# A graph attention layer on one core: the accumulators start without a product for rows that have no edge

## The chip, the cores and the metric

One core of a Trainium2 chip runs the whole layer. The metric is the device time in microseconds (us) of one execution. Before the change it is 1485.84 us, the median of three runs (1485.68 to 1487.18).

## The reference

```
h = maximum(layernorm(x), 0)                    # x: 8192 x 256, float32
Wh = h @ W_w + W_b                              # 256 x 256
e = leaky_relu((Wh @ a1)[:, None] + (Wh @ a2)[None, :], 0.2)
attention = softmax(where(adj > 0, e, -9e15), axis=1)   # adj: 8192 x 8192, int32, 0 or 1
out = x + attention @ Wh
```

A row of `adj` without a single 1 has the same value in all its columns, so its softmax is uniform and its output is x plus the mean of Wh over all 8192 nodes. Of the 8192 columns about 32 in each row hold a 1.

## The kernel before

**Names.** The 8192 output rows are handled in 8 blocks (`s`, `NS`) of 1024, each as `M` = 8 tiles (`m`) of 128 rows. The 8192 neighbours are summed over in 32 units (`k`, `NK`) of 256, each as two halves (`e`) of 128. A chunk (`g`) is 8 units, so a block has 4 chunks. The adjacency of a chunk is loaded in 8 sets, so a block has 32 sets too; set `n` of all 256 goes into slot `n % 12` of `rows8` (`R8` = 12).

**Before the blocks** (the first 100 us), x is loaded, normalised (VectorE finds the factors, GpSimd multiplies by them at L279, each 128 x 256 float32), transposed and multiplied by W on TensorE, and stored as `X16`: two float16 parts, high and low, of Wh (without its bias) times a factor of the column, with that factor in a 257th column. TensorE also forms the mean of h W (L781), and VectorE turns it into `mean` (L643 to L647).

**In the blocks**, four engines pass a unit on. ScalarE forms the products `Wt` (L362, twice 128 x 1024). VectorE applies the lower bound and the adjacency (`weights`, L656, 128 x 2048 float32, both tensor inputs in SBUF). ScalarE writes the high float16 part into `Et` (`high`, L377). VectorE writes the low part (`low`, L663, 128 x 2048, both tensor inputs in SBUF). TensorE then runs 48 products of 128 x 128 by 128 x 257 (L789): 8 tiles, 2 halves, 3 combinations of high and low parts. `Et` and `Wt` are rings of 4 units, so ScalarE's `high` waits until TensorE has read the unit four back. VectorE also transposes one set of adjacency bytes per unit (L586, 128 x 512 int32, one input), always 8 or more sets ahead of the unit that uses it.

**The order on each engine is fixed.** VectorE in a usual chunk: `weights` of the next unit, `low` of this one, a transpose. At a chunk's end its last two transposes stand together. At the first chunk of a block the order is written out (`chunk_after_last`): transposes of sets 8 and 9 of the block, `finish` of the first four tiles of the block before, `weights`, `finish` of the other four, `weights`, `low`, the transpose of set 10, and so on. `finish` (L667) takes reciprocals of the 257th column of the accumulators (L671) and adds each accumulator times its reciprocal to x in `xr` (L674, one input in PSUM and one in SBUF), a tile at a time.

**TensorE** holds the 8 accumulators in the 8 banks of PSUM. The first two and the last two units of a block go tile by tile, so that VectorE can read tile 0 while tile 1 is still being summed; before the first product into a tile, TensorE waits for VectorE's reading of it (`s_ev`) and then runs `start` (L793): a product of the constant `tiny` by `mean`, which puts 2^-100 times the mean into the accumulator and its denominator. So a row without an edge ends as the mean, and no denominator is zero.

**GpSimd** in the blocks issues the loads of the adjacency in order: `load_adj(n)` (L285, four DMAs) waits for the transpose of set n - 12, whose slot it fills. After set 27 of a block it issues the two DMAs that add the bias to `xr` (L295), each after a wait for the load of `xr`. **SyncE's queue** stores the two halves of `xr` of the last block when VectorE has read the accumulators, and loads the next x rows into `xr` when the store has landed.

Of the kernel before, what the change touches and what calls it, by code (L numbers as in the profile page):

```python
# [14 lines left out]
P = 128  # L15
# [14 lines left out]
def gat_layer(nc, x, adj, W_w, W_b, a, out):  # L30
# [48 lines left out]
    with ctx:  # L79
# [9 lines left out]
        rows8 = sb("adj_rows8", [P, R8, SQ, 4 * QP * CW], U8)  # L89
        cols8 = sb("adj_cols8", [P, 2, CW, R, 4], U8)  # L90
        xr = sb("xr", [P, 2, H, F], F32)
        tiny = sb("tiny", [P, P], BF16)
        mean = sb("mean_wh", [P, F2], F16)
        r_j = sb("r_j", [P, NB], F32)
        r_2 = r_j[:, :].rearrange("p (k e) -> p k e", e=2)
        c_j = sb("c_j", [P, NB], F32)
# [23 lines left out]
        newt = scratch[:, 1552:1568]  # L120
        rstd = scratch[:, 1568:1632]
        shift = scratch[:, 1632:1696]
        mean_hi = scratch[:, 1696:1824].bitcast(F16)
        s_t = scratch[:, 1824:1952].rearrange("p (b n) -> p b n", n=2)
        t_top = scratch[:, 1952:1984]
        t_fac = scratch[:, 1984:2016]
        h_sum = sb("h_sum", [P, KF], F32)
        mean_f = sb("mean_f", [P, F], F32)
        Wx = q_odd[:, 0:KF * F2].rearrange("p (k f) -> p k f", k=KF)
        bias = q_odd[:, KF * F2:(KF + 1) * F2]  # L130
        ident = q_odd[:, (KF + 1) * F2:(KF + 1) * F2 + P]
# [69 lines left out]
        s_fin = sem("acc_complete")  # L201
        s_rden = sem("rden_ready")
        s_ev = sem("acc_read")

# [4 lines left out]
        @block.sync  # L211
        def _(sp):
            def load_x(g):
                k, lo, hi, b = GROUPS[g]
                xk = x_in[:, k * Y:(k + 1) * Y, :].rearrange("p (w e) f -> p w (e f)", e=4)
                for q in range(NQ):
                    sp.dma_start(xk[QP * q:QP * (q + 1), lo:hi], x_cols[q, k][:, lo:hi]).then_inc(s_x[g], 16)

            load_x(0)
            for k in range(KF):  # L220
                sp.dma_start(Wx[:, k, 0:F], W_w[k * P:(k + 1) * P, :]).then_inc(s_par, 16)
            for k in range(2):
                sp.dma_start(a_row[:, k, :], a[k * F:(k + 1) * F, :].rearrange("f o -> o f").broadcast_to([P, F])).then_inc(s_par, 16)
            for g in range(1, len(GROUPS)):
                load_x(g)
            sp.dma_start(bias[:, 0:F], W_b.rearrange("(o f) -> o f", o=1).broadcast_to([P, F])).then_inc(s_bias, 16)

            def load_q(s):
                sp.dma_start(q_bc[s % 2], q_dram.ap()[s:s + 1, :].broadcast_to([P, R])).then_inc(s_q, 16)

            def load_xr(s, half):
                sp.dma_start(xr[:, half], x_rows[s, half]).then_inc(s_xr[half], 16)

            def store(s, half):
                sp.dma_start(out_rows[s, half], xr[:, half]).then_inc(s_out[half], 16)

            def store_q(q, lo, hi, done):
                sp.dma_start(q_store[q][:, lo:hi], q_j[QP * q:QP * (q + 1), 4 * lo:4 * hi].rearrange("p (z e) -> p z e", e=4)).then_inc(done, 16)

            NZ = NC * CW  # L240
            sp.wait_ge(s_qn, 1)
            store_q(0, 0, NZ // 2, s_q0)
            sp.wait_ge(s_q0, 16)
            load_q(0)
            store_q(0, NZ // 2, NZ, s_qst)
            for q in range(1, NQ):
                store_q(q, 0, NZ, s_qst)
            sp.wait_ge(s_qst, 16 * NQ)
            sp.wait_ge(s_X, NB)
            sp.wait_ge(s_mean, 1)  # L250
            for s in range(NS):
                if s + 1 < NS:
                    sp.wait_ge(s_W, NK * s + 1)
                    load_q(s + 1)
                if s:
                    for half in range(2):
                        sp.wait_ge(s_ev, M * s - H * (1 - half))
                        store(s - 1, half)
                for half in range(2):
                    if s:  # L260
                        sp.wait_ge(s_out[half], 16 * s)
                    load_xr(s, half)
            for half in range(2):
                sp.wait_ge(s_ev, M * NS - H * (1 - half))
                store(NS - 1, half)
            for half in range(2):
                sp.wait_ge(s_out[half], 16 * NS)

        @block.gpsimd
        def _(pool):  # L270
            nc.gpsimd.memset(ident, 0.0).then_inc(s_ident, 1)
            pool.wait_ge(s_ident, 1)
            nc.gpsimd.affine_select(out=ident, in_=ident, compare_op=ALU.not_equal, fill=1.0, base=0,
                                    pattern=[[-1, P]], channel_multiplier=1).then_inc(s_ident, 1)

            def normalise(b):

                pool.wait_ge(s_norm, GROUP[b] + 1)
                nc.gpsimd.tensor_scalar(x_in[:, b, :], x_in[:, b, :], rstd[:, b:b + 1], shift[:, b:b + 1],  # L279
                                        ALU.mult, ALU.add).then_inc(s_hp, 1)  # L280

            def load_quadrant(n, q):

                s, k, m = n // NSET, n % NSET // SETS, n % SETS
                pool.dma_start(rows8[QP * q:QP * (q + 1), n % R8], adj_v[s, m, k, q]).then_inc(s_rows[n % R8], 16)  # L285

            def load_adj(n):
                if n >= R8:
                    pool.wait_ge(s_T, n - R8 + 1)
                for q in range(NQ):  # L290
                    load_quadrant(n, q)

            def add_bias(s, half):
                pool.wait_ge(s_xr[half], 16 * s + 16)
                pool.dma_start(xr[:, half], W_b.rearrange("(o m f) -> o m f", o=1, m=1).broadcast_to([P, H, F]),  # L295
                               accum_op=ALU.add).then_inc(s_xb[half], 16)

            for b in range(4, NB):
                normalise(b)
                turn, at = divmod(b - 4, 3)  # L300
                if at < 2 and 2 * turn + at < NQ * SETS:
                    load_quadrant(*divmod(2 * turn + at, NQ))
            pool.wait_ge(s_q, 16)
            for n in range(SETS, NSET * NS):
                load_adj(n)
                if n % NSET == 2 * R8 + 3:
                    for half in range(2):
                        add_bias(n // NSET, half)
# [111 lines left out]
        def _(dve):  # L420
# [5 lines left out]
                dve.wait_ge(s_chain, steps[0])  # L426

            nc.vector.memset(ones, 1.0).then_inc(s_ones, 1)
            nc.vector.memset(tiny[:, :], TINY)
            step(nc.vector.memset(mean[:, :], 0.0))  # L430

            def stats(g, lo, hi):

# [206 lines left out]
            step(nc.vector.tensor_copy(X16[:, :, 0, F], c_j[:, :]))  # L640
            nc.vector.tensor_tensor(X16[:, :, 1, F], c_j[:, :], X16[:, :, 0, F], ALU.subtract).then_inc(s_den, 1)
            dve.wait_ge(s_tot, 1)
            nc.vector.tensor_copy(mean[0:1, F:F1], sc[0:1, 8:9])  # L643
            step(nc.vector.tensor_scalar(mean_f[:, :], ps_mean[:, 0:F], sc[:, 8:9], None, ALU.mult))
            step(nc.vector.tensor_copy(mean_hi, mean_f[:, :]))
            nc.vector.tensor_copy(mean[0:1, 0:F], mean_hi[0:1, :])
            nc.vector.tensor_tensor(mean[QP:QP + 1, 0:F], mean_f[QP:QP + 1, :], mean_hi[QP:QP + 1, :], ALU.subtract).then_inc(s_mean, 1)  # L647

            def weights(g, i):

# [15 lines left out]
            def finish(s, half):  # L666
# [1 line left out]
                lo = H * half  # L668
                dve.wait_ge(s_fin, M * s + (lo + H))
                dve.wait_ge(s_xb[half], 16 * s + 16)  # L670
                nc.vector.reciprocal(rden[:, lo:lo + H], acc[:, lo:lo + H, F]).then_inc(s_rden, 1)  # L671
                dve.wait_ge(s_rden, 2 * s + (half + 1))
                for m in range(lo, lo + H):
                    nc.vector.scalar_tensor_tensor(out=xr[:, half, m - lo, :], in0=acc[:, m, 0:F], scalar=rden[:, m:m + 1],  # L674
# [53 lines left out]
                    chunk(g)  # L728
            for half in range(2):
                finish(NS - 1, half)  # L730

        @block.tensor
        def _(pe):
# [50 lines left out]
            pe.wait_ge(s_X, NB)  # L784
            pe.wait_ge(s_den, 1)

            def part(m, k, e, n, last=False):

                return nc.tensor.matmul(acc[:, m, 0:F1], Et[:, 2 * (k % RING) + e, 1 if n == 2 else 0, m * P:(m + 1) * P],  # L789
                                        X16[:, 2 * k + e, 1 if n == 1 else 0, 0:F1], start=False, stop=last)  # L790

            def start(m):
                nc.tensor.matmul(acc[:, m, 0:F1], tiny[:, :], mean[:, 0:F1], start=True, stop=False)  # L793

            def first_units(s):

                pe.wait_ge(s_E, NK * s + 2)
                for m in range(M):
                    pe.wait_ge(s_ev, M * s + (m + 1 - M))
                    start(m)  # L800
                    for k in range(2):
                        for e in range(2):
                            for n in range(3):
                                ins = part(m, k, e, n)
                ins.then_inc(s_pe, 1)

            def unit(s, k):
                pe.wait_ge(s_E, NK * s + (k + 1))
                for e in range(2):
                    for m in range(M):  # L810
                        for n in range(3):
                            ins = part(m, k, e, n)
                return ins

            def last_units(s):

                pe.wait_ge(s_E, NK * s + NK)
                for m in range(M):
                    for k in range(NK - 2, NK):
                        for e in range(2):  # L820
                            for n in range(3):
                                ins = part(m, k, e, n, k == NK - 1 and e == 1 and n == 2)
                    ins.then_inc(s_fin, 1)

            for m in range(M):
                start(m)
            unit(0, 0)
            unit(0, 1).then_inc(s_pe, 1)
            for s in range(NS):
# [25 lines left out]
```

## Time and profile before

| | |
|---|---|
| median of three runs | 1485.84 us |
| profiled execution | 1486.66 us |
| its span, first to last instruction | 1484.9 us |
| TensorE matmul busy | 1450.0 us (98%) |
| VectorE busy | 1421.7 us (96%) |
| ScalarE busy | 1086.0 us (73%) |
| GpSimd busy | 605.4 us (41%) |
| mean granted TensorE clock | 0.992 of full speed |

Busy shares are unions of the recorded durations. VectorE's instructions overlap by a little at their ends, and matmuls by more, so the distance between two starts, and not the duration, says what one costs its engine.

### The profile page before, as it was taken

How to read it: one execution, taken by the hardware profiler on the slowest of the kernel's cores; microseconds unless marked ns; L12 is line 12 of the kernel's file. 1: busy time of each engine (PE TensorE's matmuls, PEld its weight loads, DVE VectorE, ACT ScalarE, POOL GpSimd, SP SyncE). 2: the span in 40 equal slices, each digit the busy share in tenths (PEclk: the TensorE clock that was granted, in tenths of full speed). 3: DMA queues.
4: the chain of work that ended last, by engine and by line, in shares of the span. 5: the costliest groups of instructions: out<-in, count | busy, mean ns of one | idle time of the engine just before them, and what ended most of it. 6: DMA issues, size and time to landing. Idle time of an engine off the chain costs nothing.

```text
span 1484.9 us, 29899 instructions
## 1 busy us (share of the span) xinstructions
PE 1450.0 (98%) x12746; PEld 1261.6 (85%) x12746; DVE 1421.7 (96%) x1263; ACT 1086.0 (73%) x1006; POOL 605.4 (41%) x1106
## 2 busy tenths in 40 slices
PE   6969999999999999999999999999999999999998
PEld 5848888888888888888888888888888888888887
DVE  8989999999999999999999999999999999999993
ACT  4768888687777777687776877777776877777771
POOL 4748444354443444354442544344432544433000
PEclk9989999999999999999999999999999999999999
DMA  9729997798778977799777977699677887788000
GB/s 215 86 26 131 98 73 55 108 82 61 51 65 102 84 51 51 85 97 69 52 64 95 86 53 51 60 117 75 48 61 102 77 61 51 51 102 70 2 1 29
DMA packets 179559, 107.53 MB, mean 72 GB/s; under 512 B 20065, under 2 KB 176353, under 8 KB 179425
## 3 DMA queue, kind: packets, MB, share of 16 engines
q0 software_dynamic: 155904, 75.56, 68.1%
q1 hardware_dynamic: 23520, 30.05, 6.9%
q8 instruction: 100, 1.64, 0.4%
q14 instruction: 35, 0.28, 0.1%
HBM read 298.45 MB, written 8.42 MB: 207 GB/s over the span
## 4 chain that ended last, share of the span: by engine, by line
PE 81%; DVE 15%; DMA 1%; issue 1%; POOL 0%; SPq 0%; ACT 0%; DVEq 0%
PE acc L789 80%; DVE work L663 4%; DVE work L656 4%; DVE xr L437 1%; DVE adj_cols L586 1%; DVE X L489 1%; DMA adj_rows<-in_adj 1%; PE acc L756 1%; PE acc L793 0%; DVE xr L448 0%; DVE xr L484 0%; DMA work<-q_rows 0%; POOL adj_rows L285 0%; DVE xr L473 0%; DVE xr L469 0%
## 5 line engine op out<-in xcount | busy, mean ns | idle before, releaser
L789 PE MATMUL acc<-X,work 128*128 128x257 f16 x12288 | 1367.6, 273 | 7.1 <-DVE work L663 7.1
L789 PEld LDWEIGHTS acc<-X,work 128*128 128x128 f16 x12288 | 1189.8, 97 | 178.8 <-DVE work L663 7.6
L285 POOL DMA_DIRECT2D adj_rows<-in_adj x1024 | 551.3, 548 | 721.4 <-DVE adj_cols L586 684.8
L377 ACT ACTIVATE work<-work 128x2048 f16<-128x2048 f32 x256 | 488.0, 1909 | 292.2 <-PE acc L789 269.8
L663 DVE SCALAR_TENSOR_TENSOR work<-work 128x2048 f16<-128x2048 f32 x256 | 585.3, 2286 | 26.6 <-ACT work L377 26.5
L656 DVE SCALAR_TENSOR_TENSOR work<-work,sigma,adj_cols 128x2048 f32<-128x2048 f32 x256 | 595.1, 2325 | 5.7 <-ACT work L362 2.2
L362 ACT ACTIVATE work<-q_odd,r_j 128x1024 f32<-128x1024 f32 x256 | 278.5, 1135 | 23.9 <-DVE work L663 23.9
L362 ACT ACTIVATE work<-work,r_j 128x1024 f32<-128x1024 f32 x256 | 278.5, 1136 | 23.4 <-DVE work L663 18.2
L586 DVE STREAM_TRANSPOSE adj_cols<-adj_rows 128x512 int32<-128x512 int32 x256 | 177.1, 701 | 1.4 <-DMA adj_rows<-in_adj 1.4
L756 PE MATMUL acc<-q_odd,adj_cols 128*128 128x258 f32 x256 | 64.4, 396 | 0.7 <-ACT adj_cols L329 0.6
L756 PEld LDWEIGHTS acc<-q_odd,adj_cols 128*128 128x128 f32 x256 | 48.0, 197 | 8.7 <-ACT adj_cols L329 2.1
L279 POOL TENSOR_SCALAR work<-work,xr 128x256 f32<-128x256 f32 x60 | 33.6, 564 | 32.4 <-DVE xr L464 31.3
L747 PE MATMUL acc<-q_odd,work 128*128 128x128 f32 x128 | 21.5, 289 | 13.2 <-ACT work L320 9.9
L747 PEld LDWEIGHTS acc<-q_odd,work 128*128 128x128 f32 x128 | 16.2, 146 | 18.4 <-issue 11.9
L437 DVE BATCH_NORM_STATS2 xr<-work 128x6 f32<-128x256 f32 x64 | 25.4, 417 | 3.9 <-DMA work<-in_x 3.7
L489 DVE SCALAR_TENSOR_TENSOR X<-acc,c_j,X 128x256 f16<-128x256 f32 x64 | 28.6, 473 | 0.0
L334 ACT ACTIVATE c_j<-xr 128x2 f32<-128x2 f32 x32 | 9.5, 296 | 25.8 <-DVE xr L484 25.3
L674 DVE SCALAR_TENSOR_TENSOR xr<-acc,rden,xr 128x256 f32<-128x256 f32 x64 | 26.6, 478 | 0.6
L339 ACT ACTIVATE X<-acc,c_j 128x256 f16<-128x256 f32 x64 | 26.8, 476 | 0.0
L329 ACT ACTIVATE adj_cols<-acc 128x256 f32<-128x256 f32 x64 | 23.4, 369 | 0.1
L295 POOL DMA_DIRECT2D xr<-in_L_gnn_W_b x16 | 21.4, 1622 | 1.0 <-issue 1.0
L793 PE MATMUL acc<-mean_wh,tiny 128*128 128x257 f16 x64 | 17.2, 291 | 2.8 <-DVE mean_wh L647 1.6
(76 smaller groups left out, 84.4 us busy)
## 6 DMA issues: line engine op xcount, KB each, us to landing
adj_rows<-in_adj POOLq DMA_DIRECT2D x1024, 64.0 KB, 4.2
xr<-in_x SPq DMA_DIRECT2D x16, 512.0 KB, 4.6
xr<-in_L_gnn_W_b POOLq DMA_DIRECT2D x16, 512.0 KB, 17.0
out<-xr SPq DMA_DIRECT2D x16, 512.0 KB, 5.4
work<-in_x SPq DMA_DIRECT2D x28, 256.0 KB, 15.1
work<-q_rows SPq DMA_DIRECT2D x4, 512.0 KB, 5.4
q_odd<-q_rows SPq DMA_DIRECT2D x4, 512.0 KB, 5.7
work<-in_x SPq DMA_DIRECT2D x8, 128.0 KB, 3.3
```

The costliest lines, as they stand in the source:

```text
L279: nc.gpsimd.tensor_scalar(x_in[:, b, :], x_in[:, b, :], rstd[:, b:b + 1], shift[:, b:b + 1], ALU.mult, ALU.add).then_inc(s_hp, 1)
L285: pool.dma_start(rows8[QP * q:QP * (q + 1), n % R8], adj_v[s, m, k, q]).then_inc(s_rows[n % R8], 16)
L362: ins = nc.scalar.mul(Wt[:, i % RING, e, :], q_bc[s % 2], r_j[:, 2 * k + e:2 * k + e + 1])
L377: nc.scalar.mul(Et[:, at:at + 2, 0, :], Wt[:, i % RING], SCALE).then_inc(s_H, 1)
L437: nc.vector.bn_stats(st[:, b % XG + n, :], x_in[:, b + n, :]).then_inc(s_bn, 1)
L489: nc.vector.scalar_tensor_tensor(out=X16[:, b, 1, 0:F], in0=ps_wh[:, b % WH, 0:F], scalar=c_j[:, b:b + 1], in1=X16[:, b, 0, 0:F], op0=ALU. ...
L586: nc.vector.transpose(rows.rearrange("p w (q r) -> p q w r", q=SQ), rows8[:, n % R8].bitcast(I32).rearrange("p q (w c) -> p q w c", w=CW)) ...
L656: nc.vector.scalar_tensor_tensor(out=slot, in0=slot, scalar=sigma[:, k:k + 1], in1=edges, op0=ALU.max, op1=ALU.min).then_inc(s_M, 1)
L663: nc.vector.scalar_tensor_tensor(out=Et[:, at:at + 2, 1, :], in0=Wt[:, i % RING], scalar=SCALE, in1=Et[:, at:at + 2, 0, :], op0=ALU.mult, ...
L747: ins = nc.tensor.transpose(ps_hT[p % 2][:, (2 * c + e) * P:(2 * c + e + 1) * P], x_in[:, b, c * P:(c + 1) * P], ident)
L756: ins = nc.tensor.matmul(ps_wh[:, b % WH, 0:F2], hT[:, p % 2, c, e * P:(e + 1) * P], Wx[:, c, :], start=(c == 0), stop=(c == KF - 1))
L789: return nc.tensor.matmul(acc[:, m, 0:F1], Et[:, 2 * (k % RING) + e, 1 if n == 2 else 0, m * P:(m + 1) * P], X16[:, 2 * k + e, 1 if n == 1 ...
```

## The change

`tiny` and the products of `start` (8 before the first block, 8 in each of the other seven) go. The first product into each accumulator now carries the start flag. `finish` raises the denominator to at least 2^-100, notes in `none` which rows had no edge, and takes the reciprocal of the raised value. GpSimd, after the loads of set 21 of the next block, takes the mean times `none` for each tile into `part_mean` and adds that to `xr`; the store waits for it. In the last block VectorE adds the mean itself after its `finish`. The mean is a plain float32 copy of TensorE's result, where five instructions stood.

```diff
@@ sync
-                        sp.wait_ge(s_ev, M * s - H * (1 - half))
+                        sp.wait_ge(s_mn, M * s - H * (1 - half))
                         store(s - 1, half)
@@ gpsimd
+            def add_mean(s):
+                pool.wait_ge(s_mean, 1)
+                for m in range(M):
+                    pool.wait_ge(s_ev, M * s + m + 1)
+                    if M * s + m:
+                        pool.wait_ge(s_mn, M * s + m)
+                    nc.gpsimd.tensor_scalar(part_mean[:, :], mean[:, :], none[:, m:m + 1], None, ALU.mult).then_inc(s_pm, 1)
+                    pool.wait_ge(s_pm, M * s + m + 1)
+                    nc.gpsimd.tensor_tensor(xr[:, m // H, m % H, :], xr[:, m // H, m % H, :], part_mean[:, :], ALU.add).then_inc(s_mn, 1)
...
                 load_adj(n)
+                if n >= NSET and n % NSET == R8 + 9:
+                    add_mean(n // NSET - 1)
@@ vector
-            nc.vector.memset(tiny[:, :], TINY)
-            step(nc.vector.memset(mean[:, :], 0.0))
...
-            nc.vector.tensor_copy(mean[0:1, F:F1], sc[0:1, 8:9])
-            step(nc.vector.tensor_scalar(mean_f[:, :], ps_mean[:, 0:F], sc[:, 8:9], None, ALU.mult))
-            step(nc.vector.tensor_copy(mean_hi, mean_f[:, :]))
-            nc.vector.tensor_copy(mean[0:1, 0:F], mean_hi[0:1, :])
-            nc.vector.tensor_tensor(mean[QP:QP + 1, 0:F], mean_f[QP:QP + 1, :], mean_hi[QP:QP + 1, :], ALU.subtract).then_inc(s_mean, 1)
+            nc.vector.tensor_copy(mean[:, :], ps_mean[:, 0:F]).then_inc(s_mean, 1)
@@ finish
-                nc.vector.reciprocal(rden[:, lo:lo + H], acc[:, lo:lo + H, F]).then_inc(s_rden, 1)
+                step(nc.vector.tensor_scalar(rden[:, lo:lo + H], acc[:, lo:lo + H, F], TINY, None, ALU.max))
+                if s:
+                    dve.wait_ge(s_mn, M * s + (lo + H - M))
+                nc.vector.tensor_scalar(none[:, lo:lo + H], rden[:, lo:lo + H], TINY, None, ALU.is_equal)
+                nc.vector.reciprocal(rden[:, lo:lo + H], rden[:, lo:lo + H]).then_inc(s_rden, 1)
@@ after the last finish
             for half in range(2):
                 finish(NS - 1, half)
+                dve.wait_ge(s_ev, M * NS - H * (1 - half))
+                for m in range(H * half, H * half + H):
+                    nc.vector.scalar_tensor_tensor(out=xr[:, half, m - H * half, :], in0=mean[:, :], scalar=none[:, m:m + 1],
+                                                   in1=xr[:, half, m - H * half, :], op0=ALU.mult, op1=ALU.add).then_inc(s_mn, 1)
@@ tensor
-            def start(m):
-                nc.tensor.matmul(acc[:, m, 0:F1], tiny[:, :], mean[:, 0:F1], start=True, stop=False)
...
-                    start(m)
-                                ins = part(m, k, e, n)
+                                ins = part(m, k, e, n, first=(k == 0 and e == 0 and n == 0))
...
-            for m in range(M):
-                start(m)
```

## Rows read from the trace of the kernel before

**Rows 1.** Waits: engine line <- what ended the wait: us in total, times, longest.
```profile
ACT work L377 <- PE acc L789: 269.8, 190, 4.2
...
PE acc L789 <- DVE work L663: 7.1, 1, 7.1
...
PE acc L793 <- DVE xr L674: 1.2, 1, 1.2
```

**Rows 2.** The chain that ended last: start us, us, what.
```profile
183.19 1.23 DVE adj_cols L586 x2
...
223.88 1.22 DVE adj_cols L586 x2
...
293.92 160.64 PE acc L789 x1452
454.67 1.33 PE acc L789 x12
456.10 1.33 PE acc L789 x12
```

**Rows 3.** Timeline (start us, us, what, [idle before]), block 0 to block 1.
```profile
282.13 0.71 DVE L586 STREAM_TRANSPOSE adj_cols<-adj_rows 128x512 int32<-128x512 int32 x1
...
282.75 0.15 DVE L671 RECIPROCAL rden<-acc 128x4 f32<-128x4 f32 x1
282.94 1.66 DVE L674 SCALAR_TENSOR_TENSOR xr<-acc,rden,xr 128x256 f32<-128x256 f32 x4
283.13 2.15 POOL L285 DMA_DIRECT2D adj_rows<-in_adj  x4 [5.18 <-DVE adj_cols L586]
...
283.57 0.27 PE L793 MATMUL acc<-mean_wh,tiny 128*128 128x257 f16 x1 [1.20 <-DVE xr L674]
...
284.51 2.34 DVE L656 SCALAR_TENSOR_TENSOR work<-work,sigma,adj_cols 128x2048 f32<-128x2048 f32 x1
...
286.77 0.18 DVE L671 RECIPROCAL rden<-acc 128x4 f32<-128x4 f32 x1
...
288.56 2.35 DVE L656 SCALAR_TENSOR_TENSOR work<-work,sigma,adj_cols 128x2048 f32<-128x2048 f32 x1
...
293.02 0.71 DVE L586 STREAM_TRANSPOSE adj_cols<-adj_rows 128x512 int32<-128x512 int32 x1
```

**Rows 4.** Timeline, VectorE, block 1: the `low` of unit 15.
```profile
353.10 2.29 DVE L663 SCALAR_TENSOR_TENSOR work<-work 128x2048 f16<-128x2048 f32 x1
```

**Rows 5.** Timeline, VectorE, block 2: the transposes of sets 22 and 23.
```profile
518.86 1.30 DVE L586 STREAM_TRANSPOSE adj_cols<-adj_rows 128x512 int32<-128x512 int32 x2
```

**Rows 6.** One line, GpSimd's normalising: duration ns min/median/max, first and last start.
```profile
L279 POOL TENSOR_SCALAR work<-work,xr x60: 544/553/1176, 15.2 to 83.6; 128x256 f32<-128x256 f32 x60
```

**Rows 7.** Timeline before the blocks: GpSimd beside VectorE with two inputs in SBUF.
```profile
29.06 0.58 POOL L279 TENSOR_SCALAR work<-work,xr 128x256 f32<-128x256 f32 x1
29.28 0.38 DVE L471 TENSOR_TENSOR xr<-xr 128x8 f32<-128x8 f32 x1
...
30.48 0.16 DVE L471 TENSOR_TENSOR xr<-xr 128x8 f32<-128x8 f32 x1
...
73.50 1.18 POOL L279 TENSOR_SCALAR work<-work,xr 128x256 f32<-128x256 f32 x1
...
73.57 0.42 DVE L573 CUSTOM_DVE_ANT_0 X<-q_odd,xr 128x256 f32<-128x256 f32 x1
...
73.91 0.42 DVE L573 CUSTOM_DVE_ANT_0 X<-q_odd,xr 128x256 f32<-128x256 f32 x1
```

**Rows 8.** Timeline, GpSimd's first steps: one waits for the other.
```profile
0.74 0.21 POOL L271 MEMSET q_odd<- 128x128 f32 x1 [0.29 <-POOLq L845]
1.19 0.29 POOL L273 TENSOR_SCALAR_AFFINE_SELECT q_odd<-q_odd 128x128 f32<-128x128 f32 x1 [0.24 <-POOL q_odd L271]
```

**Rows 9.** DMA issues: KB each, median us from issue to landing.
```profile
adj_rows<-in_adj POOLq DMA_DIRECT2D x1024, 64.0 KB, 4.2
```

**Rows 10.** Timeline: the end.
```profile
1479.77 1.66 DVE L674 SCALAR_TENSOR_TENSOR xr<-acc,rden,xr 128x256 f32<-128x256 f32 x4
```

More of the change, by code:

```diff
@@ L91, in gat_layer @@
         xr = sb("xr", [P, 2, H, F], F32)
-        tiny = sb("tiny", [P, P], BF16)
-        mean = sb("mean_wh", [P, F2], F16)
+        none = sb("rows_without_edge", [P, M], F32)
+        part_mean = sb("part_mean", [P, F], F32)
         r_j = sb("r_j", [P, NB], F32)
@@ L122, in gat_layer @@
         shift = scratch[:, 1632:1696]
-        mean_hi = scratch[:, 1696:1824].bitcast(F16)
         s_t = scratch[:, 1824:1952].rearrange("p (b n) -> p b n", n=2)
@@ L127, in gat_layer @@
         h_sum = sb("h_sum", [P, KF], F32)
-        mean_f = sb("mean_f", [P, F], F32)
+        mean = sb("mean_hw", [P, F], F32)
         Wx = q_odd[:, 0:KF * F2].rearrange("p (k f) -> p k f", k=KF)
@@ L203, in gat_layer @@
         s_ev = sem("acc_read")
+        s_pm = sem("mean_part_ready")
+        s_mn = sem("means_added")
         NPE = NK - 3
@@ L263, in _ @@
             for half in range(2):
-                sp.wait_ge(s_ev, M * NS - H * (1 - half))
+                sp.wait_ge(s_mn, M * NS - H * (1 - half))
                 store(NS - 1, half)
@@ L785, in _, with part @@
             pe.wait_ge(s_den, 1)
-            def part(m, k, e, n, last=False):
+            def part(m, k, e, n, first=False, last=False):
                 return nc.tensor.matmul(acc[:, m, 0:F1], Et[:, 2 * (k % RING) + e, 1 if n == 2 else 0, m * P:(m + 1) * P],
-                                        X16[:, 2 * k + e, 1 if n == 1 else 0, 0:F1], start=False, stop=last)
-            def start(m):
-                nc.tensor.matmul(acc[:, m, 0:F1], tiny[:, :], mean[:, 0:F1], start=True, stop=False)
+                                        X16[:, 2 * k + e, 1 if n == 1 else 0, 0:F1], start=first, stop=last)
             def first_units(s):
@@ L811, in unit @@
                         for n in range(3):
-                            ins = part(m, k, e, n)
+                            ins = part(m, k, e, n, first=(s == 0 and k == 0 and e == 0 and n == 0))
                 return ins
@@ L821, in last_units @@
                             for n in range(3):
-                                ins = part(m, k, e, n, k == NK - 1 and e == 1 and n == 2)
+                                ins = part(m, k, e, n, last=(k == NK - 1 and e == 1 and n == 2))
                     ins.then_inc(s_fin, 1)
-            for m in range(M):
-                start(m)
             unit(0, 0)
```

## The prediction, made before the changed kernel was run

> **What bounds the kernel now.** I read the waits first. TensorE waits for VectorE once at the start of the blocks (7.1 us) and once for `finish` (1.2 us), and never again [rows 1]; ScalarE waits 269.8 us for TensorE to free its ring. So TensorE bounds blocks 1 to 7. The chain of waits says the same, and shows what it costs: in the middle of a block 1452 products take 160.64 us, 110.6 ns each; at the start of a block the steps of one tile lie 1.43 to 1.44 us apart, of which 12 products are 1.33 and the product of `start` 0.11 [rows 2]. A block lasts 1536 x 0.1106 + 8 x 0.11 = 169.9 + 0.9 = 170.8 us.
>
> Then I ask how much slower VectorE could be before it takes over. In block 0 it runs without a pause: between the double transposes of two chunks lie 223.88 - 183.19 = 40.69 us [rows 2], so 162.7 us for four chunks. The two `finish` add 284.51 - 282.75 = 1.76 and 288.56 - 286.77 = 1.79 [rows 3]. VectorE needs 166.3 us a block, TensorE 170.8. VectorE has 4.5 us a block to spare, and the change draws on that from both ends.
>
> **The change, part by part.**
>
> *The products of `start`.* The first eight run while TensorE waits for the first unit: no gain. The other 56 stand in TensorE's stream: 0.9 us a block, 6.2 us in all, and TensorE's need falls to 169.9. That is the whole gain. What is late next is VectorE, with 3.6 us to spare.
>
> *The preparation.* Two memsets, and four of five small instructions on the mean, go; the first product of ScalarE waits for a DMA there, and TensorE for `low`. Zero, within 1 us either way for what TensorE's clock does when its eight early products are gone.
>
> *`finish`.* The maximum and the wait for it cost what the reciprocal and its wait cost, 282.94 - 282.75 = 0.19 us [rows 3]; the comparison stands without a wait ahead of the reciprocal, which I put at 0.1. So 0.3 us each, 0.6 a block; between 0.2 and 0.5 each. The wait on `s_mn` is for additions of a block earlier. At the first switch TensorE already waits for `finish` [rows 3]: there 0.3 us is lost directly.
>
> *The end.* VectorE adds the mean itself: four instructions behind each `finish`. The first four lie beside the last products. The second four do not: L674, of the same size, takes 1.66 us for four [rows 10], and a wait about 0.2. With the 0.3 of `finish` that is 2.1 us on the path, between 1.5 and 2.6.
>
> *SyncE's queue.* The store of a half and the load of x rows behind it come later by what GpSimd takes; they are wanted only at the next `finish`, over 100 us on. The bias DMA stands behind set 27 in GpSimd's queue and waits for that load.
>
> *GpSimd's additions.* This decides. Sixteen instructions a block, each waiting for the one before. L279, one input, 128 x 256, takes 553 ns, and once 1176 [rows 6]. What that one stood beside is the point: it started at 73.50; VectorE ran two instructions with two SBUF inputs at 73.57 and 73.91, the second starting before the first had ended, neither longer than 0.42; GpSimd ended at 74.68, 0.35 us after the second [rows 7]. It did not get in between the two. The other way round, a small L471 that takes 0.16 alone took 0.38, because it met a GpSimd instruction that ended 0.02 us before it did [rows 7]. So the two engines shut each other out where VectorE reads two inputs in SBUF, and a pair without a pause on VectorE keeps GpSimd out throughout.
>
> The Trainium skill ("SBUF — State Buffer", section "Who interferes with whom") says that the shared pair of ports is an exclusive lock and that "a DVE instruction with two SBUF inputs contends with a GpSimd instruction that reads SBUF". The rows above agree. It adds that whoever comes first has the pair for its whole instruction; by that alone a waiting addition would get in behind each VectorE instruction, which is the second case below.
>
> `weights` and `low` both read two SBUF tensors and follow each other without a pause: the one at 284.51 lasts 2.34 us and the next instruction starts 2.26 later, before its end, as in the pair [rows 3]. So I let GpSimd in only while VectorE transposes or reads the accumulators, one SBUF input each. Of an L279, about 0.3 us need the port (what was left of it behind the pair in [rows 7]), so 0.25 us pass before; the addition with two inputs I take as 0.55 of port, between 0.3 and 0.9. A wait of GpSimd for its own result costs 0.24 [rows 8]. So 0.5 us lie between the end of one and the next's asking. A transpose gives a window of 0.62 us, 282.75 - 282.13 [rows 3]: one instruction per transpose.
>
> The schedule of a block, from [rows 3]: GpSimd issues set 21 until 285.3 and then asks, while `weights` runs (until 287.1). In `finish` of the second half, 2.3 us to the next `weights`, three instructions fit. Thirteen are left. Transposes of sets 10, 11, 12 and so on each take one, twelve up to set 21. The thirteenth runs when VectorE reaches set 22. But set 22 waits for its load, the load stands behind the additions in GpSimd's queue, and it can be issued only now: 0.65 for the addition and its end, 1.65 to the start of the fourth DMA (2.15 us for four [rows 3]), 4.2 to land [rows 9]: 6.6 us on VectorE. Set 23 (in the trace of before directly behind set 22 [rows 5]) lands 2.15 later, of which 0.6 is the transpose: 1.5 more. Sum 8.1 us of standing still a block. Besides, additions with two inputs outlast some windows by 0.1 (0.5 a block), and the comparison meets one (0.15).
>
> VectorE then needs 166.3 + 0.6 + 0.65 + 8.1 = 175.7 us a block against TensorE's 169.9, and bounds the kernel.
>
> **The sum.** First switch +0.3. Blocks 1 to 6: 6 x (175.7 - 170.8) = +29.4. Block 7 has no successor to be late for: it gains 0.9 and pays what the stop costs TensorE. In block 1 `low` of unit 15 ends at 355.4 [rows 4], and TensorE starts that unit at 283.57 + 8 x 1.44 + 13 x 5.31 = 364.1 [rows 2, 3], 8.7 later; of that go 0.6 (TensorE earlier, measured from `finish`), 1.2 and 8.1, so TensorE waits about 1.2. Block 7: +0.3. End +2.1. Together +32.1 us on the execution of 1486.66 us (span 1484.9), which stands 0.8 above the median: 1517.9.
>
> **The rivals.**
>
> *GpSimd gets in at every boundary of VectorE* (not slower). For: VectorE's starts leave some 0.1 us in which neither of two instructions streams. Against: the pair in [rows 7]. Then the additions are over some 35 us after the switch and no load is late; each that falls between two long instructions delays the second by 0.4 or 0.6, each beside a transpose by next to nothing. Walking the written order: 3.3 us a block. VectorE needs 166.3 + 0.6 + 3.3 = 170.2: +0.3, 6 x -0.6, -0.9, +2.1 give -2.1, 1483.8. It decides from 3.0 us on: 1 us of delay more is 6 us.
>
> *The delay is small* (faster): the long instructions are not held up, or the additions fall into gaps. TensorE stays the bound: -6.2 + 0.3 + 2.1 = -3.8, 1482.0. Against: the L471 of 0.38 us.
>
> *One addition fits more* into `finish` or between. The last is over at set 21, load 22 is issued earlier, and VectorE waits 1.5 for each of two sets: need 171.2, +4 us, 1490. With a further 0.5 of delay 1493.
>
> *The clock.* Waits of 4 us at the switches could lower it, as after the gap ahead of the blocks; but TensorE then waits anyway: at most 2 us.
>
> The Trainium skill ("GPSIMD Engine Reference", section "Elementwise — side-by-side cycle accounting") gives 4497 ns for an addition of 2048 elements; by that an estimate for 256 is about 0.6 to 0.7 us, close to my value. With it nothing changes in the count of windows.
>
> **How the numbers follow.** The late loads: 0.36. One more fits: 0.15, half of that within 1487 to 1490. In at every boundary: 0.23, about half of it over 0.2% faster. Small delay: 0.20. Worse than my case (fewer windows caught, slower landing): 0.06. Faster by over 0.2%, about 3 us, which is what a measurement of this kernel can tell from no change: 0.30; within it 0.18; slower 0.52. The time is that of the likeliest, 1517.9, its own range 1505 to 1526. The whole range takes in the other cases: 1481.6 to 1526.
>
> **What would show it.** Right: GpSimd's additions with durations of 2 to 5 us; the last of a block near its set 22; a gap ahead of that transpose, released by the adjacency's DMA; TensorE waiting about 4 us at each switch; blocks of 175 us. For the second case: additions of some 2.5 us, all over within 40 us, and longer `weights` and `low` beside them. For the third: additions of 0.55 to 0.7 us and blocks of 169.9. It is wrong if an addition gets in between `weights` and `low`, or if load 22 is issued before VectorE arrives at its transpose.

## The result, and the profile after

The changed kernel takes 1481.83 us (median of 8 runs, 1481.17 to 1482.73) against 1486.05 us before (8 runs, 1485.59 to 1487.18): 4.2 us less, ratio 0.9971, 95% interval 0.9963 to 0.998. I had forecast 1517.9 us and slower. The time is that of the rival "the delay is small" (1482.0); the trace shows that its mechanism was not that one. It also lies inside the whole range that I gave (1481.6 to 1526), but only because that range was drawn around the rivals; this says nothing for the forecast.

The page of the changed kernel, busy time by engine:

```profile
PE 1441.5 (97%) x12682; PEld 1254.1 (85%) x12682; DVE 1440.5 (97%) x1297; ACT 1102.6 (75%) x1006; POOL 876.5 (59%) x1218
```

VectorE is busier by 18.8 us and GpSimd by 271 us, and yet the end comes sooner. The chain of waits of the changed kernel says why (start us, us, what); it answers to [rows 2] and [rows 10]:

```profile
108.42 2.21 DVE work L671
110.76 1361.64 PE acc L805 x12288
1472.91 1.67 DVE xr L686 x4
1474.60 0.48 DVE xr L745
```

One piece of TensorE, without a break from the first unit to the last. 12288 products in 1361.64 us are 110.8 ns each on the average of all blocks (110.6 in the middle of a block before); 56 products of `start` are gone. From one block's `finish` to the next lie 169.91 us, where 170.83 lay before. Behind it stand `finish`, and now the additions of L745.

The waits of the changed kernel, against [rows 1]:

```profile
ACT work L376 <- DVE work L671: 136.9, 211, 6.7
ACT work L391 <- DVE work L664: 117.2, 158, 1.5
ACT work L391 <- PE acc L805: 54.8, 42, 3.4
...
PE acc L805 <- DVE work L671: 10.7, 1, 10.7
...
DVE work L671 <- ACT work L391: 3.8, 2, 3.0
...
DVE adj_cols L598 <- DMA adj_rows<-in_adj: 0.2, 1, 0.2
```

ScalarE waited 269.8 us for TensorE; now 54.8, and 254 for VectorE (64 before). VectorE stands still no more (3.8 us behind ScalarE, 26.5 before), but TensorE waits for it only at the start. No load is late. VectorE has gone to the edge, and not over it.

Where it went: the timeline of block 2 in the changed kernel, first VectorE (L664 is `weights`, L671 is `low`), then GpSimd (L301 is the product, L303 the addition).

```profile
457.96 2.34 DVE L664 SCALAR_TENSOR_TENSOR work<-work,sigma,adj_cols 128x2048 f32<-128x2048 f32 x1
460.22 2.81 DVE L671 SCALAR_TENSOR_TENSOR work<-work 128x2048 f16<-128x2048 f32 x1
...
463.59 2.24 DVE L671 SCALAR_TENSOR_TENSOR work<-work 128x2048 f16<-128x2048 f32 x1
465.76 2.81 DVE L664 SCALAR_TENSOR_TENSOR work<-work,sigma,adj_cols 128x2048 f32<-128x2048 f32 x1
...
471.92 2.30 DVE L664 SCALAR_TENSOR_TENSOR work<-work,sigma,adj_cols 128x2048 f32<-128x2048 f32 x1
474.15 2.28 DVE L671 SCALAR_TENSOR_TENSOR work<-work 128x2048 f16<-128x2048 f32 x1
```

```profile
458.69 2.20 POOL L303 TENSOR_TENSOR xr<-xr,part_mean 128x256 f32<-128x256 f32 x1
...
463.91 2.51 POOL L303 TENSOR_TENSOR xr<-xr,part_mean 128x256 f32<-128x256 f32 x1
...
472.14 5.00 POOL L301 TENSOR_SCALAR part_mean<-mean_hw,rows_without_edge 128x256 f32<-128x256 f32 x1 [0.17 <-POOL xr L303]
...
491.73 2.57 POOL L303 TENSOR_TENSOR xr<-xr,part_mean 128x256 f32<-128x256 f32 x1
494.25 5.98 POOL L286 DMA_DIRECT2D adj_rows<-in_adj  x11
```

The addition that starts at 458.69 waits while `weights` runs, gets in when `low` should start, and `low` lasts 2.81 instead of 2.28: 0.53 us of delay. The same between `low` and `weights` at 465.76. But the product at 472.14 lets the change from `weights` to `low` at 474.15 pass, and lasts 5.00 us, until the transpose behind `low`. It is the only one of the block that does, and in all seven blocks it is the same one. The sixteen are over at 494.3, some 27 us before VectorE reaches set 22 (521.66).

Summed over the block by starts (each less the 2.26 or 2.20 between two starts in [rows 3] and after it), the delays are 0.13, 0.53, 0.48, 0.54, 0.23, 0.53 and 0.53: 3.0 us. VectorE then needs 166.3 + 0.6 + 3.0 = 169.9 us, TensorE 169.9. The `low` of unit 2 ends at 460.22 + 2.81 = 463.03; TensorE comes to that unit at 463.2, counted back from the end of its piece in the chain: 1472.4, less 0.27 for the last product's way through, less 9120 products of 0.11063 (160.64 / 1452, [rows 2]).

The busy time of blocks, in windows (us; busy of PE, PEld, DVE, ACT, POOL with instructions; granted clock, DMA share, GB/s), of the changed kernel and then of the same without GpSimd's additions (an experiment below):

```profile
454.00:625.00 171.00, 171.00 (x1548) 149.55 (x1546) 170.40 (x111) 131.23 (x98) 110.97 (x147) 1.00 0.75 72
```

```profile
454.00:625.00 171.00, 171.00 (x1548) 149.56 (x1546) 168.35 (x115) 128.66 (x98) 71.67 (x130) 1.00 0.80 73
```

The same window before had VectorE at 167.30.

### The profile page after: what moved, and what is told of

Read it like the earlier page. It is cut to its first block, busy times and chain, and to the rows that moved or that the text cites. A ratio compares the mean times of both kernels' runs of the same rounds, so it can differ in the third digit from the quotient of the medians.

```text
span 1479.7 us, 29987 instructions
## 1 busy us (share of the span) xinstructions
PE 1441.5 (97%) x12682; PEld 1254.1 (85%) x12682; DVE 1440.5 (97%) x1297; ACT 1102.6 (75%) x1006; POOL 876.5 (59%) x1218
## 4 chain that ended last, share of the span: by engine, by line
PE 93%; DVE 6%; DMA 1%; issue 0%; ACT 0%; SPq 0%; DVEq 0%; ACTq 0%
PE acc L805 92%; DVE xr L449 1%; DVE X L501 1%; PE acc L772 1%; DVE xr L460 0%; DVE xr L496 0%; DMA work<-q_rows 0%; DVE xr L485 0%; DVE xr L481 0%; DVE xr L470 0%; DVE xr L483 0%; DMA work<-in_x 0%; DVE work L664 0%; DVE work L671 0%; PE acc L763 0%
## 5 line engine op out<-in xcount | busy, mean ns | idle before, releaser
L286 POOL DMA_DIRECT2D adj_rows<-in_adj x1024 | 560.1, 719 | 443.9 <-DVE adj_cols L598 419.6
L664 DVE SCALAR_TENSOR_TENSOR work<-work,sigma,adj_cols 128x2048 f32<-128x2048 f32 x256 | 600.1, 2344 | 6.8 <-ACT work L376 3.3
L671 DVE SCALAR_TENSOR_TENSOR work<-work 128x2048 f16<-128x2048 f32 x256 | 598.4, 2338 | 3.9 <-ACT work L391 3.8
L301 POOL TENSOR_SCALAR part_mean<-mean_hw,rows_without_edge 128x256 f32<-128x256 f32 x56 | 144.3, 2576 | 8.9 <-POOL xr L303 7.5
L303 POOL TENSOR_TENSOR xr<-xr,part_mean 128x256 f32<-128x256 f32 x56 | 124.7, 2226 | 4.7
```

The lines of the kernel that those rows point to most:

```text
L301: nc.gpsimd.tensor_scalar(part_mean[:, :], mean[:, :], none[:, m:m + 1], None, ALU.mult).then_inc(s_pm, 1)
L303: nc.gpsimd.tensor_tensor(xr[:, m // H, m % H, :], xr[:, m // H, m % H, :], part_mean[:, :], ALU.add).then_inc(s_mn, 1)
L664: nc.vector.scalar_tensor_tensor(out=slot, in0=slot, scalar=sigma[:, k:k + 1], in1=edges, op0=ALU.max, op1=ALU.min).then_inc(s_M, 1)
L671: nc.vector.scalar_tensor_tensor(out=Et[:, at:at + 2, 1, :], in0=Wt[:, i % RING], scalar=SCALE, in1=Et[:, at:at + 2, 0, :], op0=ALU.mult, ...
```

## The experiments

Each was timed against the kernel before on the same chip; its median there was 1485.9 to 1486.9 us. So two versions timed on different chips can differ by up to 1 us for that reason alone; where it matters, the length of a block in the traces is given beside the time. The code shown is the part that matters; where a part is left out, the waits for it went too.

**The products of `start` alone**, taken out of the kernel before:

```diff
-                    start(m)
-                                ins = part(m, k, e, n)
+                                ins = part(m, k, e, n, first=(k == 0 and e == 0 and n == 0))
```

> The kernel before with the products of start left out and the flag on the first product, and nothing else (a row without an edge would be divided by zero; the input has none). Theory A (TensorE's stream is the whole gain): 56 products of 0.11 us go, so 6.2 us less than the kernel before, about 1479.8 us, and 2 us less than the changed kernel. Rival B (part of the gain is an earlier start of the blocks, since the trace after has no wait of 1.2 us at the first switch): the products alone give 4 to 5 us, about 1481.5 us. If the wait of 1.2 us at the first switch stays in this trace, it belongs to the kernel before's preparation; if it is gone, it varies from run to run.

Measured: 1480.45 us (1480.17 to 1481.17), against 1486.42 (11 runs): 6.0 us less, ratio 0.9961, interval 0.9948 to 0.9973. Theory A. TensorE's wait at the first switch [rows 1] is 0.7 us here:

```profile
PE acc L789 <- DVE xr L674: 0.7, 1, 0.7
```

It goes with VectorE's waits for the adjacency in block 0: 1.2 us with 1.4 of those in the profiled execution before, 0.7 with 0.7 here, and none with 0.2, both in the changed kernel and in the kernel before with one microsecond more for VectorE (below). That last one has the old preparation, so the wait varies from run to run and the change of the preparation is not needed to explain it. The profiled executions before and after differ by 5.2 us, the medians by 4.2; the wait is of about the size that is left between the two, but nothing else links them.

**Without GpSimd's additions**:

```diff
-                if n >= NSET and n % NSET == R8 + 9:
-                    add_mean(n // NSET - 1)
```

> The changed kernel without GpSimd's additions in the first seven blocks (the mean of a row without an edge is left out there). Theory A (VectorE's slack hides what GpSimd takes from it): the same time as the changed kernel within 0.5 us, about 1481.8 us; long VectorE instructions back at 2.35 us at most; VectorE finishes the low part of unit 2 about 0.7 us ahead of TensorE instead of 0.05, and waits appear on VectorE by the end of a block. Rival C (the additions cost time at each block's start, where the lead is nil): 0.1 to 0.5 us a block less, 1 to 3.5 us in all, 1478.5 to 1481 us.

Measured: 1482.04 us (7 runs, 1481.18 to 1482.53), no less than the changed kernel, and a block lasts 169.95 us, as in the changed kernel. The additions cost nothing as they stand. VectorE waits for ScalarE again:

```profile
DVE work L669 <- ACT work L389: 18.8, 74, 3.0
```

**Without the additions at the end**:

```diff
-                dve.wait_ge(s_ev, M * NS - H * (1 - half))
-                for m in range(H * half, H * half + H):
-                    nc.vector.scalar_tensor_tensor(... in0=mean[:, :], scalar=none[:, m:m + 1] ...).then_inc(s_mn, 1)
```

> The changed kernel without VectorE's additions behind the last block's finish (the mean of a row without an edge is left out in the last block). Theory A: the second four additions are the whole cost of the end, 1.7 us and a short wait: 1.8 to 2.0 us less than the changed kernel, about 1479.9 us. Rival D (the output's DMA, not the engine, sets the end): less than 1 us.

Measured: 1480.06 us (1479.92 to 1480.28): 1.8 less than the changed kernel's 1481.83, 2.0 less than the run without GpSimd's additions beside it. Theory A, not D.

**One microsecond more for VectorE**, on the changed kernel and on the one before:

```diff
+                if half == 1 and s < NS - 1:
+                    for v in range(3):
+                        nc.vector.bn_stats(spare[:, 3 * s + v, :], mean[:, :])
```

> The changed kernel with three BN_STATS of 128 x 256 (one input; 0.33 us from start to start before the blocks) behind the finish of the second half in blocks 1 to 7: 1.0 us more for VectorE a block, nothing else. Theory E (the change has used up VectorE's slack: its need is 169.9 us a block, TensorE's too): every microsecond shows, less what the longer pause without two inputs gives GpSimd: 0.5 to 1.0 us a block, 3.5 to 7 us over the changed kernel, 1485.5 to 1489 us. Rival F (slack is left, the lead of 0.05 us at unit 2 is only where the queue happens to settle): under 1 us more.

> The kernel before with the same three BN_STATS a block. Theory E: VectorE has 4.5 us a block to spare there, so the same time within 0.5 us, about 1486.3 us. Rival G (VectorE bounds the kernel before too, as the equal busy shares suggest): 7 us more, 1493 us.

Measured: 1486.34 us (10 runs) on the changed kernel, 4.5 more than without; 1486.41 us (10 runs) on the kernel before, ratio 0.9998 (0.9988 to 1.0007). So 1 us a block is free before and costs 0.65 us a block after; in the trace a block lasts 170.63 us instead of 169.91. In the changed kernel with it TensorE waits for `low` once in each of seven blocks besides the start:

```profile
PE acc L810 <- DVE work L672: 14.2, 8, 10.8
```

**Every addition twice**:

```diff
+                    nc.gpsimd.tensor_tensor(xr[:, m // H, m % H, :], xr[:, m // H, m % H, :], part_mean[:, :], ALU.add).then_inc(s_m2, 1)
+                    pool.wait_ge(s_m2, M * s + m + 1)
+                    nc.gpsimd.tensor_scalar(part_mean[:, :], mean[:, :], none[:, m:m + 1], None, ALU.mult).then_inc(s_pm, 1)
```

> The changed kernel with every addition of GpSimd done twice: 32 instructions a block (a row without an edge would get its mean twice; the input has none). Theory E: another ten instructions fit before VectorE reaches set 22 and delay it by 2.6 us; the rest run then and only after them is the load of set 22 issued, which stands still for some 13 us: 15 us a block, about 1580 us, with VectorE's longest waits on the adjacency's DMA. Rival H (the additions are hidden whatever their number): 1482 us. Between them, 1500 to 1515 us, would say that only the delay of 2.6 to 4.3 us counts and no load is late.

Measured: 1618.11 us (1617.73 to 1619.45), ratio 1.0886. The mechanism is the one expected, the size 19.5 us a block where I had 15. The longer `weights` and `low` sum to 5.6 us a block, as I had it (3.0 and 2.6); what was too small is the standing still, 16.9 us instead of 13, because set 23 is late too. 166.3 + 0.6 + 5.6 + 16.9 = 189.4, and a block lasts 189.7. (The mean granted clock is 0.958 here and 0.992 in the changed kernel, with TensorE waiting in each block; the sum closes without it.) Its timeline, VectorE at sets 22 and 23 and then GpSimd:

```profile
542.03 2.82 DVE L676 SCALAR_TENSOR_TENSOR work<-work 128x2048 f16<-128x2048 f32 x1
558.49 0.71 DVE L603 STREAM_TRANSPOSE adj_cols<-adj_rows 128x512 int32<-128x512 int32 x1 [13.64 <-DMA adj_rows<-in_adj]
562.49 0.71 DVE L603 STREAM_TRANSPOSE adj_cols<-adj_rows 128x512 int32<-128x512 int32 x1 [3.29 <-DMA adj_rows<-in_adj]
```

```profile
542.80 2.84 POOL L306 TENSOR_SCALAR part_mean<-mean_hw,rows_without_edge 128x256 f32<-128x256 f32 x1
545.72 0.73 POOL L308 TENSOR_TENSOR xr<-xr,part_mean 128x256 f32<-128x256 f32 x1
546.62 0.92 POOL L302 TENSOR_SCALAR part_mean<-mean_hw,rows_without_edge 128x256 f32<-128x256 f32 x1 [0.17 <-POOL xr L308]
...
549.46 0.72 POOL L308 TENSOR_TENSOR xr<-xr,part_mean 128x256 f32<-128x256 f32 x1
550.12 4.93 POOL L287 DMA_DIRECT2D adj_rows<-in_adj  x9
```

VectorE stands at the transpose of set 22 from 544.85 to 558.49; meanwhile the rest of the additions run, now 0.73 and 0.92 us each since nothing shuts them out; the load is issued from 550.1 and lands 8 us later. This is the late load of my forecast, in a kernel with twice the additions.

One more thing stands in this trace. The fourth addition of a block begins to wait 0.65 to 0.67 us after the start of `weights` in each of the seven blocks. In four it gets in before `low`, which then lasts 2.8 us; in three it misses the change, `low` lasts 2.28, and the addition itself 4.48:

```profile
668.78 4.48 POOL L308 TENSOR_TENSOR xr<-xr,part_mean 128x256 f32<-128x256 f32 x1
```

So an addition can miss a change too: 3 of the 66 that waited at one from `weights` to `low` here, none of 28 in the changed kernel.

**One input each.** The addition becomes a second product, so that all 16 instructions are of the kind on which I had built the forecast:

```diff
-                    nc.gpsimd.tensor_tensor(xr[:, m // H, m % H, :], xr[:, m // H, m % H, :], part_mean[:, :], ALU.add)
+                    nc.gpsimd.tensor_scalar(part_two[:, :], part_mean[:, :], none[:, m:m + 1], None, ALU.mult)
```

> The changed kernel with the addition replaced by a second product of a tile and a scalar, so that all 16 instructions of GpSimd have one tensor input (the mean isn't added; rows without an edge stay x). In the trace after, each of seven blocks has one such instruction of 5.0 us, which waited under weights and was not let in when low followed. Theory I (an instruction with one input that waits under weights misses that boundary, one with two inputs does not; one that waits under low gets in): about half of the instructions last near 5 us, and low is never longer than 2.3 us. Rival J (it is a matter of timing in that one place): durations near 2.5 us, low of 2.6 us at several places.

Measured: 1486.65 us in one run. Lighter instructions, and 4.8 us slower; a block lasts 170.7 us instead of 169.9. GpSimd's second product and VectorE's `low` (min/median/max ns), and VectorE's wait for the adjacency:

```profile
L304 POOL TENSOR_SCALAR part_two<-part_mean,rows_without_edge x56: 917/4510/4967, 286.9 to 1360.0; 128x256 f32<-128x256 f32 x56
```

```profile
L672 DVE SCALAR_TENSOR_TENSOR work<-work x256: 2240/2281/2291, 108.6 to 1458.4; 128x2048 f16<-128x2048 f32 x128
```

```profile
DVE adj_cols L599 <- DMA adj_rows<-in_adj: 21.3, 8, 3.3
```

VectorE at sets 20 to 23 of block 2, and GpSimd's loads behind the last product:

```profile
510.66 0.70 DVE L599 STREAM_TRANSPOSE adj_cols<-adj_rows 128x512 int32<-128x512 int32 x1
...
515.71 0.70 DVE L599 STREAM_TRANSPOSE adj_cols<-adj_rows 128x512 int32<-128x512 int32 x1
...
520.77 0.70 DVE L599 STREAM_TRANSPOSE adj_cols<-adj_rows 128x512 int32<-128x512 int32 x1
524.75 0.71 DVE L599 STREAM_TRANSPOSE adj_cols<-adj_rows 128x512 int32<-128x512 int32 x1 [3.28 <-DMA adj_rows<-in_adj]
```

```profile
506.48 4.96 POOL L304 TENSOR_SCALAR part_two<-part_mean,rows_without_edge 128x256 f32<-128x256 f32 x1
511.39 12.98 POOL L287 DMA_DIRECT2D adj_rows<-in_adj  x24
```

`low` is never held up; `weights` is, at four places a block (2.45 to 2.56 us). The products miss 56 changes from `weights` to `low` of 56, eight in a block, and half of the 112 last 4.5 us or more, up to the next transpose. The last is over at 511.4, at the transpose of set 20. Set 22 is then still in time; set 23 is late by about 3 us, since the loads issued one behind the other take some 9 us to land and not the 4.2 of [rows 9]. The chain that ended last has it so in another block, seven issues and then the landing of set 23's last:

```profile
1023.51 3.73 POOL adj_rows L287 x7
1027.24 9.03 DMA adj_rows<-in_adj
```

So GpSimd is shut out as in my forecast, and a load is late by it as there; but the queue is free two transposes before set 22, the late set is the next one, and the size is near that of my rival "one addition fits more" (it had 171.2 us a block).

**Two inputs each**:

```diff
-                    nc.gpsimd.tensor_scalar(part_mean[:, :], mean[:, :], none[:, m:m + 1], None, ALU.mult)
+                    nc.gpsimd.tensor_tensor(part_mean[:, :], mean[:, :], mean[:, :], ALU.subtract)
```

> The changed kernel with the product replaced by mean minus mean, so that all 16 instructions have two tensor inputs (what is added is zero for every row; the mean of a row without an edge is left out). Theory I: none lasts 5 us; every boundary lets one in, low and weights of 2.8 us. VectorE is delayed by 0.5 us at each boundary without a transpose, about 4 us a block instead of 3, so TensorE waits about 1 us a block: 1488 us. Rival J: one of 5 us a block stays, and the time is 1482 us.

Measured: 1485.01 us (10 runs, 1484.65 to 1486.4), 3.2 over the changed kernel; a block lasts 170.45 us. None lasts longer than 2.73 us:

```profile
L301 POOL TENSOR_TENSOR part_mean<-mean_hw x56: 613/2532/2727, 283.8 to 1334.6; 128x256 f32<-128x256 f32 x56
```

Theory I was right in what it foresaw, with half its price. But one input and a scalar per partition go together in it, so I took them apart.

**One input, constant scalar**:

```diff
-                    nc.gpsimd.tensor_scalar(part_mean[:, :], mean[:, :], none[:, m:m + 1], None, ALU.mult)
+                    nc.gpsimd.tensor_scalar(part_mean[:, :], mean[:, :], 0.0, None, ALU.mult)
```

(and so for the second product.)

> The version with 16 one-input products on GpSimd, whose scalar is now the constant 0.0 instead of a value per partition (no mean is added). Theory K (the number of tensor inputs decides who gets in between weights and low): durations near 4.9 us where the instruction waits under weights, and low never over 2.3 us, as with the scalars per partition. Rival L (the scalar per partition, which GpSimd reads from SBUF first, takes the turn, and the tensor has to wait for the next): none over 2.8 us, low of 2.5 us at several places, about 3 us less than 1486.7 us.

Measured: 1481.77 us in one run, 4.9 less than with the scalars per partition; the chips of the two runs differ by 1.0 us in the kernel before, but the blocks agree, 169.95 us instead of 170.7. Nothing of GpSimd lasts longer than 2.72 us now, and `low` is held up, by 0.2 us at a time:

```profile
L304 POOL TENSOR_SCALAR part_two<-part_mean x56: 850/2318/2718, 286.5 to 1335.7; 128x256 f32<-128x256 f32 x56
```

```profile
L672 DVE SCALAR_TENSOR_TENSOR work<-work x256: 2241/2284/2486, 108.4 to 1453.4; 128x2048 f16<-128x2048 f32 x128
```

Theory K, and with it the count of inputs, falls. What rival L foresaw came: of the products without a scalar per partition all 28 that waited at a change from `weights` to `low` got in, and with it none of 56. For these products the scalar per partition makes the difference. It isn't the only condition, as the additions that missed in the doubled version show.

**VectorE's scalar instead**:

```diff
-                nc.vector.scalar_tensor_tensor(out=slot, in0=slot, scalar=sigma[:, k:k + 1], in1=edges,
+                nc.vector.scalar_tensor_tensor(out=slot, in0=slot, scalar=2.0 ** -30, in1=edges,
```

> The version with 16 one-input products on GpSimd, and weights with the constant 2^-30 for its scalar instead of sigma per partition (the lower bound of the weights is left out; no mean is added). Theory K: as before, low stays under 2.3 us. Rival M (VectorE's scalar per partition in weights is what shuts GpSimd out at its end): GpSimd gets in between weights and low, low of 2.5 us, no instruction of GpSimd over 2.8 us.

(This stands on the version with 16 products with a scalar per partition, and leaves out the lower bound, so its output is not that of the layer.)

Measured: 1498.94 us in one run. Rival M falls: GpSimd's instructions still reach 4.9 us, 56 of 63 miss the change from `weights` to `low`, and VectorE waits 52.1 us for the adjacency. `low` is held up at one place of each block (2.49 us at most), so theory K's "under 2.3" fails too.

It is slower than with `sigma` because the products are shut out more often: the last is over at 515.8 in block 2 instead of 511.4, and sets 22 and 23 are both late (4.0 and 3.3 us), with blocks of 173.1 us. The trace shows where. A product that first waits under `low`, with `weights` next, got in at the one such place of each block where `weights` read `sigma` (seven of seven), and with the constant in its place missed it (seven of seven). So VectorE's scalar seems to help a product in when it belongs to the instruction about to start. One place in a block is little to rest this on, and no further run tests it.

**A version that beats both**: the changed kernel, with the old `start` and `finish` in the last block alone, where the additions behind `finish` go; the old preparation of the mean comes back for it.

```diff
                     pe.wait_ge(s_ev, M * s + (m + 1 - M))
+                    if s == NS - 1:
+                        start(m)
...
+                if s == NS - 1:
+                    nc.vector.reciprocal(rden[:, lo:lo + H], acc[:, lo:lo + H, F]).then_inc(s_rden, 1)
```

> A version that computes everything: the changed kernel in the first seven blocks, and in the last block the product of start and the old finish. Theory A: TensorE gains 48 products instead of 56 (0.9 us back), the end gains 1.9 us and 0.1 to 0.3 us of finish: 1.2 us less than the changed kernel, about 1480.6 us, 5.3 us under the kernel before. Rival B or C, by which TensorE's stream is not the only term: no less than the changed kernel.

Measured: 1480.73 us (1480.54 to 1480.98), ratio to the kernel before 0.9962 (0.995 to 0.9975); no run of the changed kernel was as fast. 1.1 us under its median, as expected: 0.9 us of products in TensorE's stream for 1.8 to 2.0 us of additions behind it.

## Why the prediction was wrong, point by point

*What bounds the kernel, and the slack.* Right. TensorE's stream bounds it; by my rows 4.5 us a block were VectorE's to spare. The runs fit: the 3.6 us that the change adds to VectorE (0.6 and 3.0), with a limit lower by 0.9, cost nothing, and one further microsecond was free before and not after.

*The products.* Right: 6.2 us forecast, 6.0 measured alone.

*Preparation, `finish`, end.* Right: 0, 0.6 a block (453.44 - 451.42 = 2.02 instead of 1.76, 457.96 - 455.83 = 2.13 instead of 1.79), 2.1 forecast and 1.8 to 2.0 measured. The 0.3 us at the first switch was not paid: TensorE did not wait there in the profiled execution.

*GpSimd's additions: this step failed.* "So I let GpSimd in only while VectorE transposes or reads the accumulators." I drew it from one pair [rows 7], in which an L279 did not get in between. But L279 multiplies by one scalar per partition and adds another. With such a scalar an instruction misses the change from `weights` to `low`, as the version with 16 of them shows; the addition of the change has none, and gets in, 28 times of 28. Whether its scalars are also why L279 missed in [rows 7] no run tests: its pair was another kind of VectorE instruction, 0.42 us long, with a read of the accumulator (0.09 us) between the two. What failed is that I carried it over. Eight of the sixteen are such additions, and that takes the queue from one instruction per transpose to nearly one per long VectorE instruction. Thirteen windows were not needed, the last addition was over at 494.3, and the 8.1 us of standing still did not exist.

*The late load.* The mechanism is real, and stands where I had it, behind the additions in GpSimd's queue; it needs the additions to last long enough. With the change's mixture they don't. With 16 scalar ones they end at set 20 and set 23 is late (about 3 us a block), with 32 instructions both sets are (17 us). My terms for it were too small: 6.6 us (6.5 by its own parts) took 4.2 us for the landing, and from the issue of set 22 to its transpose lie 558.49 - 550.12 = 8.4 us in the doubled version, where I had 5.9; set 23 adds 3.3, where I had 1.5. Had the thirteenth addition run at set 22, the standing still would have been some 12 us and not 8.1.

*The second case* described what happened: additions of some 2.5 us, over within 40 us, longer `weights` and `low`. I had given it 0.23, and a delay of 3.3 us against a threshold of 3.0. Measured are 3.0, which is the threshold itself, so its time became that of the third case: 6.0 less by the products and 1.8 to 2.0 more at the end make 4.0 to 4.2 less, and 4.2 is measured. That its time fell on the third case's and not 1.8 us higher hung on 0.3 us a block.

*The trust in the skill.* The Trainium skill's rule ("SBUF — State Buffer", "Who interferes with whom"), that whoever comes first has the pair for its whole instruction, pointed at the second case; I set it aside for one row. For who gets in, the runs mostly bear it out where the instruction has no scalar per partition (3 of 66 additions missed in the doubled version), and not where it has one. The delay is less than GpSimd's whole instruction: 0.53 us for an addition of 0.73, 0.20 for a product of 0.85.

## What to carry to other kernels

Before a pair of rows is made into a rule for new instructions, compare the operands: a scalar per partition was enough to change who gets in, and by that which engine pays. Work given to GpSimd beside a VectorE that reads two SBUF inputs is paid by VectorE, here 0.2 to 0.5 us for each that gets in between two of them, and is free only up to VectorE's slack against the engine that bounds; reckon that slack, and look for what is queued behind on GpSimd: a load that comes late there can cost more than the instructions themselves. A cost in the stream of the bounding engine and the same cost behind its end are exchangeable: compare them block by block, as the last version does.

## What the runs showed of the hardware that I had not expected

- A waiting GpSimd addition of 128 x 256 (0.73 us alone) goes in between two VectorE instructions that overlap by some 0.08 us, and the second lasts 0.53 us longer. It does not always: with the same timing to 0.02 us, the doubled version has it get in four times and miss three. A product with a constant scalar (0.85 alone) costs 0.20.
- With a scalar per partition the product takes 0.92 us alone and can last 5.0 us beside VectorE, by missing one change. Under `low`, before `weights`, such products got in while `weights` had a scalar per partition itself (21 of 21 in the changed kernel and the version with 16). That the scalar is fetched in a turn of its own would fit; no run shows it directly.
- L279, with two scalars per partition and its output in place, takes 0.55 us; L301, with one, 0.92. This stays open.
- GpSimd's wait for its own result costs 0.17 us here, not 0.24.
- A load of the adjacency issued right behind others landed some 9 us after its issue (median of all 1024 in the changed kernel 9.5 us), where the median before was 4.2.
